# Attention on one core: the transfer that turns the denominators moves from SyncE's queue to ScalarE's

## The reference

```
energy = jnp.einsum('bhqd,bhkd->bhqk', q, k)
att = jax.nn.softmax(energy, axis=-1) / D ** 0.5
out = jnp.einsum('bhqk,bhkd->bhqd', att, v)
out = out @ Wp.T + bp
```

## Time and profile before

| | us |
|---|---|
| median of 3 executions | 1863.22 |
| the profiled execution | 1859.63 |
| its span | 1857.5 |
| PE busy in the span | 1810.5 (97%) |
| DVE busy | 1254.3 (68%) |
| ACT busy | 834.5 (45%) |
| POOL busy | 1217.6 (66%) |

### The profile page before, as it was taken

How to read it: one execution, slowest core, us unless ns; L and a number is a source line. 1 busy time by engine, 2 the same in 40 slices (tenths; PEclk the granted TensorE clock), 3 DMA queues, 4 the chain that set the end, 5 groups by cost and what they waited for, 6 DMA issues and landing times. The chain is left out here.

```text
span 1857.5 us, 27080 instructions
## 1 busy us (share of the span) xinstructions
PE 1810.5 (97%) x9510; PEld 1211.9 (65%) x9510; DVE 1254.3 (68%) x1986; ACT 834.5 (45%) x1545; POOL 1217.6 (66%) x679
## 2 busy tenths in 40 slices
PE   8989999999999999999899999999999999999997
PEld 4678888888888788888555545555555555554376
DVE  4655655655645575665877777777777777777288
ACT  3213123123123122222366666666666666666465
POOL 2665465465465242342488888888888888898665
PEclk9999999999999999999999999999999999999899
DMA  7410100100103657685777787878777877775796
GB/s 269 121 35 23 57 34 23 56 34 23 56 1 114 209 181 247 211 256 205 193 157 184 179 180 176 186 176 185 176 184 175 187 179 180 181 162 123 211 386 267
DMA packets 135373, 287.10 MB, mean 155 GB/s; under 512 B 23984, under 2 KB 41520, under 8 KB 127200
## 3 DMA queue, kind: packets, MB, share of 16 engines
q1 hardware_dynamic: 102996, 200.10, 35.3%
q0 software_dynamic: 9264, 66.11, 17.5%
q10 hardware_dynamic: 23008, 19.54, 3.3%
HBM read 134.68 MB, written 84.19 MB: 118 GB/s over the span
## 5 line engine op out<-in xcount | busy, mean ns | idle before, releaser
L1619 DVE TENSOR_REDUCE at_mrow<-banks 128x1 f32<-128x512 f32 x976 | 594.2, 681 | 162.5 <-PE banks L1465 162.4
L1715 POOL TENSOR_TENSOR at_sums<-at_probs 128x2048 f32<-128x2048 f32 x127 | 596.7, 4698 | 88.3 <-DMA at_sums<-at_sums 70.8
L1599 ACT ACTIVATE at_probs<-banks 128x512 f32<-128x512 f32 x1024 | 518.4, 624 | 179.9 <-PE banks L1483 174.9
L1465 PE MATMUL banks<-early_ks,early_qs 96*128 96x512 f32 x976 | 406.3, 416 | 8.4 <-DVE at_mrow L1619 4.6
L1483 PE MATMUL banks<-early_qs,early_ks 98*128 98x512 f32 x1024 | 409.4, 418 | 1.8 <-ACT at_probs L1599 1.8
L1465 PEld LDWEIGHTS banks<-early_ks,early_qs 96*128 96x128 f32 x976 | 184.7, 189 | 138.7 <-DVE at_mrow L1619 85.8
L1483 PEld LDWEIGHTS banks<-early_qs,early_ks 98*128 98x128 f32 x1024 | 193.7, 190 | 108.7 <-ACT at_probs L1599 84.5
L1495 PE MATMUL banks<-at_probs,at_v 128*32 128x512 f32 x2048 | 252.5, 611 | 1.7 <-DMA at_v<-v_scratch 1.7
L66 PE MATMUL banks<-l_nt,l_weights 128*128 128x512 f32 x768 | 179.2, 394 | 5.4 <-DVEq L1193 4.3
L657 ACT ACTIVATE l_gt<-banks,mod 128x512 f32<-128x512 f32 x60 | 45.1, 777 | 300.2 <-PE banks L526 263.9
L66 PE MATMUL banks<-l_ht,l_weights 128*128 128x512 f32 x768 | 177.4, 390 | 1.9 <-issue 1.9
(11 more groups left out here) (147 smaller groups left out, 2155.2 us busy)
## 6 DMA issues: line engine op xcount, KB each, us to landing
at_sums<-at_sums POOLq DMA_DIRECT2D x63, 1024.0 KB, 8.0
qk_scratch<-qk_out SPq DMA_DIRECT2D x64, 512.0 KB, 6.0
early_ks<-qk_scratch SPq DMA_DIRECT2D x48, 512.0 KB, 4.9
early_qs<-qk_scratch SPq DMA_DIRECT2D x96, 256.0 KB, 5.5
attn_scratch<-at_out SPq DMA_DIRECT2D x32, 512.0 KB, 7.3
o_a<-attn_scratch SPq DMA_DIRECT2D x32, 512.0 KB, 12.7
chunk_in<-x SPq DMA_DIRECT2D x8, 1024.0 KB, 5.4
v_scratch<-qk_v ACTq DMA_DIRECT2D x32, 256.0 KB, 3.1
```

Source lines behind the costliest of these rows:

```text
L1465: pe.matmul(em[n % 3][:], qs[0:96, slot, half, j, c * P:(c + 1) * P], ks[0:96, slot, j, keys * CH:(keys + 1) * CH], start=True, stop=True) ...
L1599: nc.scalar.activation(probs[:, i % 4, j, :], et[n % 3][:], ACT.Exp).then_inc(exp_done, 1)
L1619: nc.vector.tensor_reduce(mrow[:, half, keys, u:u + 1], em[n % 3][:], AX.X, ALU.max).then_inc(max_done, 1)
L1715: nc.gpsimd.tensor_tensor(into, probs[:, a], probs[:, a + 1], ALU.add).then_inc(pair_ready, 1)
```

## The change

`spread_den` leaves SyncE's program and enters ScalarE's. ScalarE copies the denominators after step 3 and step 11, as before, and issues the transfer after the exponentials of step 5 and step 13, one pair later. The two waits go with it (that the copy is done; that the inversion of the same half one group earlier has read `den_c`). Nothing else changes: the same bytes, the same 31 transfers, the same semaphores for their landing.

```
             def group(g, slot, nth=None, ...):        # SyncE
                 fetch(0)
                 if not first:
-                    spread_den(g - 1, 1)
                     store(g - 1, 0)
                 place_neg(g, slot, 1)
...
                 fetch(2)
-                spread_den(g, 0)
                 if not first:
                     store(g - 1, 1)
...
+            def spread_den(g, half):                  # ScalarE
+
+                act.wait_ge(den_taken, halves(g, half))
+                if not (isinstance(g, int) and g == 0):
+
+                    act.wait_ge(rden_ready, halves(g, half) - 2)
+                act.dma_start(den_c[:, half],
+                              den_sb[0:P:HD, half].rearrange("j (r c) -> j r c", c=DW)).then_inc(den_spread[half], 16)
...
                     if i == KC + 3:
                         take_den(g, 0)
+                    if i == 5 and not first:
+                        spread_den(g - 1, 1)
+                    if i == KC + 5:
+                        spread_den(g, 0)
```

More of the change, by code:

```diff
@@ L1389, in place_neg @@
                     sp.dma_start(dst, neg_t[:, part]).then_inc(negm_loaded, 16)
[L1391 to L1399, removed]
             def widen_rden(g, half):
```

## The result

The changed kernel takes 2068.65 us (median of 5 runs, 2065.92 to 2073.14) against 1863.3 us before in the same session: ratio 1.1103, 95% interval 1.1082 to 1.1124. It is 205 us slower. The forecast was slower, 1976 us with a range up to 2030: the direction and the mechanism held in the main, the size did not.

The account below looks back on a forecast made before the run. TensorE, busy for 97% of the span, was taken to bound the kernel. Stops 93, clock 20 and end 3 us made 116 on top of 1859.6: 1976 us; own range 1922 to 2029, 8-in-10 range 1866 to 2030.

Parts of the forecast that it names:

- SyncE gains nothing: SyncE loses one issue of 0.61 us and a wait, but its store and `place_neg` start no sooner: gain 0.
- ScalarE's issue is hidden: Issue and two waits fit into ScalarE's 2.18 us idle time between the exponentials: cost 0.
- VectorE's wait would stop TensorE at its fourth M: Reductions start 3.95 us later in the mean, less 0.36 slack: TensorE stands 3.6 us in each of 29 halves.
- the time to land: Small transfer, from ScalarE's issue to landing beside `at_sums`: 6.05 us, the middle of 5.0 and 7.1.
- the clock: Lower granted clock for the value products behind each stop: 0.7 us per half, 20 us in all.
- given back: At the next half's start TensorE's weight load no longer waits for `place_neg`: 0.36 us less per half.
- The chain of the inverted denominators: SyncE's write, the loads and GpSimd's multiplication after the inversion: cost 0; if hidden by nothing, 2.7 us on GpSimd.
- The first rival: Own queue gets a turn after one row of `at_sums`; lands after 3.0 us, 1865 us; chance 14%.
- The second and the third rival: Second: lands after 1.9 us as if idle, 1854 us, 8%; third: after 3.0 to 4.8 us, 1865 to 1920, 6%.
- second reading: The rows a DMA engine moves for `at_sums` form one packet, which the small transfer must wait out.

Follow-up runs that it names:

- the run with the fill: The changed kernel with 16 more products, overwritten unread, ahead of TensorE's fourth M in pairs 3 and 7: 2019.56 us, ratio 1.0835 to the kernel before.

## Why the prediction was right in kind and wrong in size

- That SyncE gains nothing, that ScalarE's issue is hidden (0.53 us against an idle time of 2.18), and that VectorE's wait would stop TensorE at its fourth M, once in each of 29 halves: shown, by the timeline and the 29 waits. ScalarE's issue even ran 0.14 us ahead of its last exponential of the pair, so it came about 0.8 us sooner than forecast; it was still behind `at_sums`.
- **The first failed step: the time to land.** "Above: it lands when the 1 MB transfer of `at_sums` does", and so "I take the middle of 5.0 (rows 7) and 7.1: 6.05 us". Measured 8.0, outside the upper bound. Of the 2 us between, 0.8 are only the issue, which came that much sooner and did not make it land sooner; told from the issue of `at_sums`, the forecast put the landing at 7.9 us (upper bound 9.0), and it came at 9.1. What the bound left out is the store, 512 KB, issued 1.1 us later on the other queue: the small transfer lands a median of 1.3 us after `at_sums`. With the store out of the way it lands 7.7 us after the issue of `at_sums`, and TensorE's stop is 3.67 us, against the 3.6 of the forecast. With the store it is 5.04: 29 x 1.4 = 40 us that the sum did not have.
- **The second: the clock.** "Bounds 0 and 1.44 us per half; I take half, 0.7, so 29 x 0.7 = 20 us." That priced the block of value products alone. These did lose 20 us, but that the half of the bounds was right for them is luck: the blocks behind the stops took from 1.92 to 3.64 us. The rest of the front, which stands between the stop and them, was put at nothing without a reason; its products take 0.63 us instead of 0.40, and it lost 52 us, nearly all of them to the clock by the run with the fill.
- A third step failed by less: what was "given back". The wait of the weight load for `place_neg` did go (up to 1740 us; before and after):

```profile
PEld banks L1465 <- DMA early_qs<-at_neg_t: 13.3, 28, 0.9
```
```profile
PEld banks L1453 <- DMA early_qs<-at_neg_t: 0.4, 1, 0.4
```

  But the weight load overlaps TensorE's products, and from the value products to the next half TensorE saved 3 us in all, not 29 x 0.36 = 10.
- The chain of the inverted denominators cost nothing of its own, as forecast: it is written at 1631.27, loaded from 1633.42 on, and GpSimd waits for it once, 5.4 us, against 5.6 us in three waits before.
- The sum against the 209 us by which the span grew, in us:

| | forecast | measured |
|---|---|---|
| stops at the fourth M, less what is given back | 93 | 144 - 3 |
| rest of the front behind the stop | 0 | 52 |
| value products behind the stop | 20 | 20 |
| all else (other pairs, last group, end) | 3 | -4 |
| sum | 116 | 209 |

- The first rival (a turn beside `at_sums` after one row of it) is refuted by landing times of 6 to 8 us in three kernels and by the records: 116 rows went by without a piece. The second and the third rival fall with the same times. What spoke for the first, "other queues do get turns", was misread: in the kernel before, too, the store of 1215.66 moved nothing from 1215.7 to 1219.7 (99 records, all of `at_sums`). The Trainium skill's rule ("DMA: Bandwidth & Descriptors", Queues, rings and completion order), a round of the queues by whole packets, fits in its second reading: the small transfer waits out what `at_sums` has under way. The records show rows and pieces, not how an engine groups them.

## What to carry to other kernels

When a small transfer is moved, look first at which large transfers are under way at its new time: here some 2 us of lateness made it land 5 to 6 us later, since it fell from ahead of one large transfer to behind it. A queue of its own did not help here, and added a rival that the old queue's order had kept behind. Price a stop of TensorE with the clock over everything that runs until it is back, not over one block. And price what an engine gets back by its own idle time: a wait of the weight load is not yet one of the products.

## What the runs showed of the hardware that was not expected

- A transfer of 8 KB on an otherwise empty queue took 8.0 us with 1 MB under way on a second queue and 512 KB on a third, 6.6 without the 512 KB, and 2.5 with a quarter of the 1 MB and the 512 KB still there.
- Between the issue of the small transfer and 1627.9, 4.8 us, the DMA engines moved rows of `at_sums` and nothing else, though two more queues had work.
- ScalarE's issue at 1623.10 came ahead of the start, at 1623.24, of an exponential that stands before it in the program; all 31 did so, by 0.1 to 0.2 us.
- 16 products of no use in each stop, 3.8 us, made the kernel 49 us faster.
